# Constants, table loads, closing waits and sign products moved between engines in a graph-and-experts kernel

## What is computed

```python
x = x + _L0_gnn_ref(_layernorm(x), adj, ...)   # U, eigenvectors of the normalized Laplacian of adj:
                                               # U @ (relu((U.T @ x) @ W1 + b1) @ W2 + b2)
x = x + _L0_ffn_ref(_layernorm(x), ...)        # 8 experts, the two best of each token, softmax over the two
x = x + _L1_gnn_ref(_layernorm(x), adj, ...)   # two graph layers, then four LSTMs over windows of 1 to 4 nodes
x = x + _L1_ffn_ref(_layernorm(x), ...)        # gelu(x @ W1), softmax gate over 8, only the best expert's output
```

## Time and profile before

| | us |
|---|---|
| median of three executions | 1464.8 (1462.3 to 1465.9) |
| the profiled execution, own time | 1469.6 |
| its span | 1467.9 |
| PE busy | 1120.2 (76%) |
| DVE busy | 839.6 (57%) |
| ACT busy | 749.9 (51%) |
| POOL busy | 557.5 (38%) |

### The profile page before, as it was taken

How to read it: one execution, slowest core, us unless ns; L and a number is a source line. 1 busy time by engine, 2 the same in 40 slices (tenths; PEclk the granted TensorE clock), 3 DMA queues, 4 the chain that set the end, 5 groups by cost and what they waited for, 6 DMA issues and landing times. The chain is left out here.

```text
span 1467.9 us, 28039 instructions
## 1 busy us (share of the span) xinstructions
PE 1120.2 (76%) x6333; PEld 829.7 (57%) x6334; DVE 839.6 (57%) x3907; ACT 749.9 (51%) x2074; POOL 557.5 (38%) x855
## 2 busy tenths in 40 slices
PE   2444422638862899999976998999999689929995
PEld 1223322527752799999974664445544345429995
DVE  4777798986775333344548993444444568622221
ACT  3555543623440566666644775665555466505552
POOL 3666614710367773045427710000000006644553
PEclk9999965568865899999997999999999899959998
DMA  9500000000012333233322200000000002243330
GB/s 257 136 1 1 1 1 0 1 1 5 24 44 65 101 122 94 69 103 103 103 69 51 53 8 1 0 0 0 0 1 0 4 1 85 87 130 102 105 103 26
DMA packets 85702, 75.57 MB, mean 51 GB/s; under 512 B 13207, under 2 KB 74848, under 8 KB 85613
## 3 DMA queue, kind: packets, MB, share of 16 engines
q1 hardware_dynamic: 71788, 44.64, 11.0%
q0 software_dynamic: 13824, 29.98, 6.5%
HBM read 41.72 MB, written 33.37 MB: 51 GB/s over the span
## 5 line engine op out<-in xcount | busy, mean ns | idle before, releaser
L1207 POOL DMA_INDIRECT z<-spent,seats x64 | 63.0, 985 | 393.4 <-DVE spent L1328 375.7
L1673 ACT ACTIVATE c_H<-ps,c_b 128x128 f32<-128x128 f32 x576 | 156.9, 383 | 98.4 <-PE ps L1719 98.4
L2234 PE MATMUL ps<-BIG,spent 128*128 x364 | 157.2, 581 | 3.4 <-ACTq L2247 3.4
L1719 PE MATMUL ps<-ZS,c_w 128*128 128x128 f32 x1152 | 143.3, 278 | 3.5 <-ACT ZS L1662 2.4
L1705 PE MATMUL ps<-spent,c_H 128*128 x1152 | 141.1, 276 | 0.0
L1719 PEld LDWEIGHTS ps<-ZS,c_w 128*128 128x128 f32 x1152 | 136.6, 195 | 4.6 <-ACT ZS L1662 3.0
L1705 PEld LDWEIGHTS ps<-spent,c_H 128*128 128x128 f32 x1152 | 135.2, 193 | 0.0
L2234 PEld LDWEIGHTS ps<-BIG,spent 128*128 128x128 f32 x364 | 70.1, 193 | 85.4 <-issue 85.4
L2242 PE MATMUL ps<-e_hs,spent 128*128 128x512 f32 (+1 forms) x256 | 110.0, 572 | 0.0
L856 POOL DMA_INDIRECT z<-BIG,spots x64 | 63.3, 990 | 113.3 <-DVE spots L973 95.9
L1573 POOL DMA_INDIRECT c_rows<-y,seats x64 | 60.4, 944 | 116.9 <-DMA y<-c_ys 62.2
(11 more groups left out here) (511 smaller groups left out, 2658.0 us busy)
## 6 DMA issues: line engine op xcount, KB each, us to landing
BIG<-z SPq DMA_DIRECT2D x72, 129.0 KB
ZB<-z SPq DMA_DIRECT2D x144, 64.0 KB
y<-c_ys SPq DMA_DIRECT2D x72, 128.0 KB
spent<-in_L_ffn_W_dram SPq DMA_DIRECT2D x1, 2048.0 KB
spent<-in_L_ffn_W_dram SPq DMA_DIRECT2D x8, 256.0 KB
w_dn<-in_L_ffn_Wd_dram SPq DMA_DIRECT2D x8, 256.0 KB
z<-BIG,spots POOLq DMA_INDIRECT x128, 2.2
z<-j_padding SPq DMA_DIRECT2D x9, 129.0 KB, 3.0
```

Source lines behind the costliest of these rows:

```text
L1207: pool.indirect_dma_start(z, bass.IndirectOffsetOnAxis(ap=k.seats[:, 0, n:n + 1], axis=0), k.R[:, row(n), :], None, bounds_check=E * STRID ...
L1673: act.activation(H[u][:, c, h * P:(h + 1) * P], UP[u][c // 2][:, o:o + P], ACT.Gelu, bias=b1[u][h][:, c:c + 1]).then_inc(gelu, 1)
L1719: pe.matmul(UP[u][c // 2][:, o:o + P], w1[u][h][:, c * P:(c + 1) * P], ZT[u][:, h * P:(h + 1) * P], start=True, stop=True).then_inc(up, 1)
L2234: last = pe.matmul(view(k.ps[4 * u + j], wide, lanes), k.w_ihT[:, w, :], state(i, u, s, p, wide, lanes), start=True, stop=(s == 0))
```

## The change

- **Head.** On GpSimd the select that makes `ident` moves ahead of the other constants; the add of the bias rows moves into step 12 (`ROWS_AT`) of its 62. VectorE's constants move ahead of its wait for `A`, and most are issued without waiting for each other; the copy of `L0` moves behind `x`. TensorE transposes `A` twice, once for ScalarE and once into `ps[3]` for VectorE, and waits for the constants only afterwards. ScalarE begins with a square root of a column that nobody reads, and takes the real one before the copy of `adjsum`. X has a semaphore for each quarter, and ScalarE waits for a quarter before its first tile.
- **Passes.** The products of signs move from GpSimd to VectorE: those of the first three leaves four steps of the recursion behind the leaf, the last behind `ratio`.
- **Tables.** Activations of one column into `k.warm`, which nobody reads: Gelu behind the exponential of gate 0, Gelu at the very start of ScalarE's part of gate 1, Sigmoid behind `floor` in gnn1.
- **End.** The waits for the scattered output move from GpSimd to SP.

```diff
@@ spectrum, gpsimd
             pool.memset(ident[:, :], 0.0).then_inc(s_pool, 1)
             pool.memset(pivot[:, :], 0.0).then_inc(s_pool, 1)
+            pool.wait_ge(s_pool, 2)
+            pool.affine_select(out=ident[:, :], in_=ident[:, :], compare_op=ALU.not_equal, fill=1.0, base=0,
+                               pattern=[[-1, P]], channel_multiplier=1).then_inc(s_pool, 1)
...
-            pool.wait_ge(s_pool, 3)
-            pool.wait_ge(s_rows, 16 * 5)
-            pool.tensor_tensor(rows[0:SKIPS * GATES, :], rows[0:SKIPS * GATES, :], rows2[:, :], ALU.add).then_inc(s_sum, 1)
             for i in range(STEPS):
+                if i == ROWS_AT:
+                    pool.wait_ge(s_rows, 16 * 5)
+                    pool.tensor_tensor(rows[0:SKIPS * GATES, :], rows[0:SKIPS * GATES, :], rows2[:, :],
+                                       ALU.add).then_inc(s_sum, 1)
...
-                    a, b = LEAVES[c], LEAVES[c + 1]
-                    pool.wait_ge(s_signs, turn * (len(LEAVES) - 1) + c + 1)
-                    pool.tensor_tensor(changes[:, a + 1:b + 1, :], signs[:, a:b, :], signs[:, a + 1:b + 1, :],
-                                       ALU.mult).then_inc(s_changes, 1)
@@ spectrum, scalar
+            act.wait_ge(s_pool, 2)
+            act.activation(k.warm[:, :], pivot[:, 0:1], ACT.Sqrt)
             act.wait_ge(s_turned, 1)
...
+            act.wait_ge(s_square, 1)
+            act.activation(root[:, :], half_B[:, :], ACT.Sqrt).then_inc(s_rooted, 1)
             act.wait_ge(s_rowsum, 1)
...
-            act.wait_ge(s_square, 1)
-            act.activation(root[:, :], half_B[:, :], ACT.Sqrt).then_inc(s_rooted, 1)
...
             def token_mean(n):
+                if n % (TILES // 4) == 0:
+                    act.wait_ge(s_x[n // (TILES // 4)], 16)
...
-            act.wait_ge(s_x, 16 * 4)
@@ spectrum, tensor
+            pe.transpose(ps[0][:, 0:N], A[:, :], ident[0:N, 0:N]).then_inc(s_turned, 1)
+            pe.transpose(ps[3][0:N, 0:N], A[:, 0:N], ident[0:N, 0:N]).then_inc(s_turned, 1)
             pe.wait_ge(s_const, CONSTS)
-            pe.transpose(ps[0][:, 0:N], A[:, :], ident[0:N, 0:N]).then_inc(s_turned, 1)
@@ spectrum, vector
-            dve.wait_ge(s_turned_sb, 2)
-            dve.wait_ge(s_const, CONSTS)
-            link(tt_(junk[0:N, :], A[:, 0:N], ps[0][0:N, 0:N], ALU.add))
+            dve.wait_ge(s_pool, 3)
+            link.put(dve.memset(nudge, NUDGE))
...
+            link.put(dve.tensor_copy(M[:, N:P], ident[0:N, 0:N]))
+            dve.wait_ge(s_turned, 2)
+            link(tt_(junk[0:N, :], A[:, 0:N], ps[3][0:N, 0:N], ALU.add))
...
+            tt_(M[:, 0:N], half_B[0:N, :], scale[0:N, :], ALU.mult).then_inc(s_matrix, 1)
...
+            link.put(dve.tensor_copy(L0[:, :], M[:, 0:N]))
@@ counts
+                def turned(c):
+                    a, b = LEAVES[c], LEAVES[c + 1]
+                    dve.wait_ge(s_signs, first + c + 1)
+                    tt_(changes[:, a + 1:b + 1, :], signs[:, a:b, :], signs[:, a + 1:b + 1, :],
+                        ALU.mult).then_inc(s_changes, 1)
                 for n in range(2, HALF + 1):
+                    if n - 4 in LEAVES[1:]:
+                        turned(LEAVES.index(n - 4) - 1)
...
                 tt_(ratio[:, :], ratio[:, :], minors[:, HALF, :], ALU.mult).then_inc(s_tail, 1)
+                turned(len(LEAVES) - 2)
@@ gate0_parts, scalar
         act.activation(ex[:, :], ex[:, :], ACT.Exp).then_inc(s_exd, 1)
+        act.activation(k.warm[:, :], k.prio[:, 0:1], ACT.Gelu)
@@ experts_out_parts, sync and gpsimd
         rounds(sp, fetch, NT, DEPTH + 4, 0)
+        for b in range(DEPTH):
+            sp.wait_ge(placed[b], 16 * HALVES * len(range(b, NT, DEPTH)))
...
-        for b in range(DEPTH):
-            pool.wait_ge(placed[b], 16 * HALVES * len(range(b, NT, DEPTH)))
@@ gnn1, scalar
             act.activation(floor[:, :], GATE[0][:, 0:P], ACT.Copy, scale=-1.0).then_inc(floored, 1)
+            act.activation(k.warm[:, :], k.prio[:, 0:1], ACT.Sigmoid)
```

More of the change, by code:

```diff
@@ L61 @@
 AT_ROOT = GROUPS - 1
+ROWS_AT = 12
 DEPTH = 8
@@ L165, in spectrum @@
         raw = [k.BIG[:, u * 2048:(u + 1) * 2048].rearrange("q (w d) -> q w d", d=P) for u in range(2)]
-        (s_adj, s_rows, s_raw, s_x, s_const, s_pool, s_turned, s_turned_sb, s_offd, s_deg, s_square, s_rooted,
+        (s_adj, s_rows, s_raw, s_const, s_pool, s_turned, s_turned_sb, s_offd, s_deg, s_square, s_rooted,
          s_matrix, s_row, s_length, s_inverse, s_ycol, s_half, s_sign, s_xs, s_xcol, s_beta, s_q, s_ntyc, s_scaled, s_xm, s_ym, s_mean, s_var, s_scale,
@@ L170, in spectrum @@
          s_ritz_row, s_factor, s_refined) = (sem("h_" + n) for n in (
-             "adj rows raw x const pool turned turned_sb offd deg square rooted matrix row length inverse "
+             "adj rows raw const pool turned turned_sb offd deg square rooted matrix row length inverse "
              "ycol half sign xs xcol beta q ntyc scaled xm ym mean var scale std z za tokens tokens_sb zw zw_sb diag diag_row "
@@ L174, in spectrum @@
              "factor refined").split())
+        s_x = [sem(f"h_x{q}") for q in range(4)]
         ch, s_load = k.ch, k.s_load
@@ L183, in _ @@
                 r = slice(q * TILES // 4, (q + 1) * TILES // 4)
-                sp.dma_start(k.X[:, r, :], x_tok[:, r, :]).then_inc(s_x, 16)
+                sp.dma_start(k.X[:, r, :], x_tok[:, r, :]).then_inc(s_x[q], 16)
             for dst, src in loads["rows"](rows, rows2):
@@ L205, in _ @@
                 ins.then_inc(s_const, 1)
-            pool.wait_ge(s_pool, 2)
-            pool.affine_select(out=ident[:, :], in_=ident[:, :], compare_op=ALU.not_equal, fill=1.0, base=0,
-                               pattern=[[-1, P]], channel_multiplier=1).then_inc(s_pool, 1)
             pool.memset(pivot[:, N:N + 1], 1.0).then_inc(s_const, 1)
@@ L467, in _ @@
             tt_, ts_, stt = dve.tensor_tensor, dve.tensor_scalar, dve.scalar_tensor_tensor
-            dve.wait_ge(s_turned_sb, 2)
-            dve.wait_ge(s_const, CONSTS)
-            link(tt_(junk[0:N, :], A[:, 0:N], ps[0][0:N, 0:N], ALU.add))
+            dve.wait_ge(s_pool, 3)
+            link.put(dve.memset(nudge, NUDGE))
+            link.put(dve.memset(OFF[:, :], 0.0))
+            link.put(ts_(minus[:, :], ident[:, 0:N], -1.0, None, ALU.mult))
+            for r, o in ((slice(0, N), slice(N, P)), (slice(N, P), slice(0, N))):
+                link.put(dve.tensor_copy(swap[:, r], ident[:, o]))
+                link.put(tt_(both[:, r], ident[:, r], ident[:, o], ALU.add))
+            link.put(dve.memset(upper_half[:, N:P], 0.0))
+            link(dve.memset(lower_half[:, 0:N], 0.0))
+            link.put(dve.tensor_copy(upper_half[:, 0:N], both[:, 0:N]))
+            link.put(dve.tensor_copy(lower_half[:, N:P], both[:, N:P]))
+            link.put(dve.tensor_copy(M[:, N:P], ident[0:N, 0:N]))
+            dve.wait_ge(s_turned, 2)
+            link(tt_(junk[0:N, :], A[:, 0:N], ps[3][0:N, 0:N], ALU.add))
             link(tt_(offd[:, :], A[:, 0:N], ident[0:N, 0:N], ALU.mult))
@@ L491, in _ @@
             link(stt(out=half_B[0:N, :], in0=junk[0:N, :], scalar=-0.5, in1=half_B[0:N, :], op0=ALU.mult, op1=ALU.add))
[L492 to L497, removed]
-                link.put(dve.tensor_copy(swap[:, r], ident[:, o]))
-                link.put(tt_(both[:, r], ident[:, r], ident[:, o], ALU.add))
-            link.put(dve.memset(upper_half[:, N:P], 0.0))
-            link(dve.memset(lower_half[:, 0:N], 0.0))
-            link.put(dve.tensor_copy(upper_half[:, 0:N], both[:, 0:N]))
-            link(dve.tensor_copy(lower_half[:, N:P], both[:, N:P]))
-            dve.tensor_copy(M[:, N:P], ident[0:N, 0:N]).then_inc(s_matrix, 1)
+            tt_(M[:, 0:N], half_B[0:N, :], scale[0:N, :], ALU.mult).then_inc(s_matrix, 1)
             dve.wait_ge(s_xm, 1)
@@ L569, in counts @@
                 leaf = turn * (len(LEAVES) - 1)
+                first = leaf
+                def turned(c):
[3 more added lines that the diff above has]
+                        ALU.mult).then_inc(s_changes, 1)
                 for n in range(2, HALF + 1):
+                    if n - 4 in LEAVES[1:]:
+                        turned(LEAVES.index(n - 4) - 1)
                     for h, c in enumerate(parts):
@@ L2362, in gnn_ffn_kernel @@
         k.prio = sb("prio", [P, E])
+        k.warm = sb("warm", [P, 1])
         k.LG = sb("LG", [P, TILES, E])
```

## The result

The changed kernel takes 1451.1 us (median of four executions, 1448.4 to 1453.3). The kernel before, run beside it, took 1465.35 us (1462.3 to 1466.7). The ratio is 0.9906, with a 95% interval of 0.9884 to 0.9927: faster, by 14.2 us or just under 1%, where 15.9 us had been forecast.

The account below looks back on a forecast made before the run. No engine was taken as busy throughout; the bound was a sequence of stages, most with a barrier, set by the last-ending waits. Terms 9.0 + 2.3 + 0.6 + 0 - 1.4 + 5.4 = 15.9 took 1464.8 to 1448.9 us, range 1443 to 1456.

Parts of the forecast that it names:

- Head: Start of the kernel up to and through the 62 steps: 9.0 us gained, bounds 7.5 to 9.5.
- Passes: Three counting passes: 9.7 us of holds removed, less 5.4 for products and 2.0 for waits; gain 2.3, bounds -1 to 5.
- (a): Head: VectorE waits for two transposes instead of ScalarE's copies, starting at about 4.25 instead of 5.28; gain 1.0 us.
- (b): Head: square root table loaded early and the real root ahead of the adjsum copy, shortening VectorE's wait; gain 1.5 us.
- (c): Head: with the constants moved earlier, `x` is taken at 13.6 instead of 15.55, after the matrix; gain 2.0 us.
- (d): Head: step 0 starts when `x` is ready, 15.82, instead of when all of X has landed, 19.85; gain 4.0 us.
- (e): Head: step 0 lasted longer than the next because GpSimd came late from its wait for the bias rows; gain 0.7 us.
- (f): Head: the add of 0.45 us moves into step 12, where GpSimd waits for `x`; loss taken as 0.2 us.
- Gelu of gate 1: Opening of gate 1: the unhidden table load and its activation delay ScalarE's first copy; loss 1.4 us, bounds -1.5 to 0.
- Tail: Kernel's end: without the output waits, GpSimd's closing DRAIN starts behind the last issue; gain 5.4 us, bounds 1.5 to 5.4.
- A stage already ends so: Tail: an earlier stage's DRAIN ended 5.3 us after its last issue, so the closing one would too, at 1462.3, not 1467.7.
- R1: Rival at the tail: the closing DRAIN keeps its 9.19 us whatever precedes it; gain 1.5 there, 1452.8 us; chance 0.27.

Follow-up runs that it names:

- run 1: The changed kernel, with ScalarE waiting for all four quarters of X ahead of step 0, as before the change: 1457.6 us.
- run 4: The changed kernel, with TensorE's token products behind the last count and ScalarE's last signs ahead of the tokens' copy in passes 2 and 3: 1447.3 us.
- run 6: The changed kernel, with the Gelu of one column moved behind the first three copies of gate 1: 1450.5 us.
- run 5: The changed kernel, with an unneeded GpSimd instruction (two-input bf16, one-input bf16, two-input f32) behind each of three leaves of pass 1: 1453.0 us, one execution.

## Why the prediction was right, and where it wasn't

**Head, 9.0 forecast, 9.0 measured.** Term by term: (a) VectorE's start 1.0, measured 1.25; (b) sum to matrix 1.5, measured 1.36 (7.31 to 5.95); (c) matrix to `x` 2.0, measured 1.96 (2.96 to 1.00); (d) from `x` to step 0 4.0, measured 4.05 (4.30 to 0.25); (e) and (f) together 0.5, measured 0.37, and that agreement is luck: steps 0 and 1 became 1.5 shorter where 0.7 was forecast, the step that holds the add 0.2 longer as forecast, and a further 0.9 went in other steps, most of it in steps 6, 15 and 22 (counted from 0). There one instruction of ScalarE or VectorE starts 0.3 us later than before; the forecast had no such term, and its cause isn't shown. What the sum doesn't say, run 1 does: these terms don't stand by themselves. The wait for X was the last to end, so it alone decided whether (a) to (c) counted. With it left in, 7.7 of the 9.0 are gone. The forecast had priced its removal at 4.0 behind the others, which is right for the whole and would be wrong for anyone who drops a part.

**Passes, 2.3 forecast, 3.2 measured.** From a pass's first instruction (L567) to the ratio the recursion got 1.98, 2.23 and 1.99 us shorter, although nine products now stand in it. From the start of such a product to the start of the next instruction 0.40 us pass (640 wide) or 0.30 (448), 3.3 in all. So 9.5 us of holds went, where 9.7 was forecast. The durations of all twelve products add up to 5.1 us (5.4 forecast), but each begins before its predecessor has ended, so VectorE loses less than that; the estimate from the Trainium skill (VectorE: DVE Perf Modes, "The perf-mode tier table") of 0.49, 0.39 and 0.32 us stands against 0.486, 0.382 and 0.337 measured, so the page was nearer than the middle of two far rows. The waits at the ends of passes 2 and 3 grew by 1.62 and 1.35, together 2.97 and with the last product of each (0.37 and 0.33) in it, where 2.0 was charged. 9.5 - 3.3 - 3.0 = 3.2. The thread that was charged is the right one, as run 4 shows; the products were priced too high and the wait too low, and the two errors partly cancel.

**Gelu of gate 0, 0.6 forecast, 0.64 measured** (5.91 to 5.27 between the first two tiles' copies; 4.98 to 5.27 in all kernels that have the change). As forecast, the second four Gelus wait for TensorE, 0.50 us. This part wasn't undone by itself. **Sigmoid of gnn1, 0 forecast**: the stage took 136.4 us before, 135.65 in the changed kernel's profile and 136.4 to 137.6 in the twelve kernels run afterwards, all with that part untouched; no gain can be read from it.

**Gelu of gate 1, -1.4 forecast.** The copy came 1.39 later, and run 6 gives 1.36 back when the load moves into an idle stretch. The profile of the changed kernel alone could mislead: its first real Gelu came 22.44 us behind the barrier instead of 23.80. TensorE's matmuls ahead of it, eight at L1498, took 5.41 us instead of 6.75, since the granted clock went from 0.5 to 1.0 earlier among them, 3.5 us after the first one's start instead of 6.2. The loss is seen in what follows, the gate's last scattered write.

**Tail, 5.4 forecast, 1.5 measured: the step that failed, though the total came out near.** It was "A stage already ends so": the DRAIN of 7.46 at 744.1 was read as a fixed 5.3 behind the last issue, and it isn't fixed. The 9.19 of the kernel before and the 9.20 behind the last issue now are the same cost, whether waits stand ahead of it or not. R1, with 0.27, was what happened here, at its price, and the DRAIN of 9 us had been named as a sign of being wrong. Its argument ("it follows scattered writes") doesn't carry either, for behind 64 scattered writes of gate 1 it is 5.28.

With the measured sizes the sum is 9.0 + 3.2 + 0.6 - 1.4 + 1.5 = 12.9, and the medians differ by 14.2 in one session and 11.9 in the other (1464.65 to 1452.7). The predicted 1448.9 lies 2.2 under the 1451.1: 3.9 too much at the tail, 0.9 too little in the passes, the rest within what executions differ by. R1's 1452.8 is nearer to the 1451.1 than the forecast is, so the range was met with the leading case for the tail wrong.

## What to carry to other kernels

Where several waits end one behind the other at the same instruction, only the last one has a price; undo the parts singly before you credit any. Before a stall is put on an instruction, read what stands ahead of the awaited one in its engine's queue: a turn of two orders gave more here than moving the products did. And a cost at a block's end that looks fixed may be, as in the last block here, a debt that grows with the work before it; pay it where the engine idles.

## What the runs showed that was not expected

- GpSimd's DRAIN in the last block: 1.48 us behind 8 indirect transfers, 2.8 behind 32, 5.9 behind 72, 9.2 behind 136 (9.2 even where GpSimd had waited for all the landings first).
- GpSimd's one-input instruction held VectorE for 0.46 us at its start and not afterwards; its two-input ones for 69 to 85% of their length (0.60 of 0.87, 1.14 of 1.45, 1.18 of 1.39). Two products at once suffer alike: in run 5 VectorE's own product of 0.34 us took 1.51 beside one of GpSimd's.
- Stages with the same code differ between executions, by 5.5 us in gate 0's stage and by 2.8 in the last. The granted clock of TensorE over 10 us from the first Gelus of the last experts (columns: window, length, busy times of PE, PEld, DVE, ACT, POOL, then the clock), of the changed kernel, then of the same kernel again:

```profile
1297.00:1307.00 10.00, 9.01 (x58) 7.96 (x58) 1.01 (x4) 5.87 (x15) 1.10 (x2) 0.97 0.46 122
```

```profile
1301.30:1311.30 10.00, 9.22 (x37) 7.37 (x37) 0.50 (x3) 3.91 (x10) 0.00 (x0) 0.62 0.46 124
```

With the clock at 0.62, the stage took 2.8 us more to VectorE's end (295.75 against 292.97). The kernel before showed 0.65 there in its profile. In gate 0 the first 65 us had 0.84 before, 0.84 in the second and 0.88 in the first profile of the changed kernel, and 0.94 in three of its variants, and with them the stage took 427.5, 425.1, 422.9 and 419.5 to 419.7 us. The same 0.84 stands beside two lengths, so this clock isn't all of it. Stage by stage the 21.3 us between the two profiled spans are 12.1, 4.7, 0.75, 1.4, 0.9 and, behind VectorE's end, 1.5. The parts of the change explain 12.9 of them; the rest lies in stages whose code is the same or nearly so, and it is why a part of 1 to 2 us had to be read from the trace.
